# Last four tiles of a transformer and S4D layer on one core: three tiles scaled in a row, the residual sums shared out anew between VectorE and GpSimd, and the stores regrouped

## The reference

```
x = x + attention(layernorm(x))        # causal, 256 wide, with its own layernorm and residual
x = x + ffn(layernorm(x))              # first pass of the same ffn
x = x + s4d(layernorm(x))              # convolution over 512 time steps, B = 2 of them as tensor rows
x = x + ffn(layernorm(x))              # second pass

def ffn(x):                            # 256 -> 768 -> 256
    gate = silu((x @ fp8(gate_w)) * gate_scale)
    up   = (x @ fp8(up_w)) * up_scale
    return ((gate * up) @ fp8(down_w)) * down_scale
```

## Time and profile before

| | us |
|---|---|
| median of 3 runs | 124.89 (124.87 to 124.93) |
| the profiled execution | 124.83 |
| its span, first to last instruction | 123.0 |

### The profile page before, as it was taken

How to read it: one execution, slowest core, us unless ns; L and a number is a source line. 1 busy time by engine, 2 the same in 40 slices (tenths; PEclk the granted TensorE clock), 3 DMA queues, 4 the chain that set the end, 5 groups by cost and what they waited for, 6 DMA issues and landing times.

```text
span 123.0 us, 2126 instructions
## 1 busy us (share of the span) xinstructions
PE 116.2 (94%) x682; PEld 78.3 (64%) x682; DVE 96.1 (78%) x229; ACT 77.5 (63%) x147; POOL 83.7 (68%) x165
## 2 busy tenths in 40 slices
PE   5997999999999999999999999999999999999970
PEld 5885468658668758744678645667445479756650
DVE  0499999919865878768797988999899994797582
ACT  2235079695776367947966359786389666589700
POOL 2246569999999888888633388869876782037721
PEclk9999999999999999999999999999999999999997
DMA  3999930000000000000000000000000000000505
GB/s 94 302 308 365 337 101 8 0 0 0 0 0 0 3 8 0 0 0 0 0 0 0 5 0 0 0 3 5 0 0 0 3 0 5 0 0 0 171 0 171
DMA packets 5682, 5.80 MB, mean 47 GB/s; under 512 B 1140, under 2 KB 5160, under 8 KB 5672
## 3 DMA queue, kind: packets, MB, share of 16 engines
q1 hardware_dynamic: 4648, 5.52, 13.5%
q10 hardware_dynamic: 960, 0.15, 0.7%
q0 software_dynamic: 64, 0.02, 0.2%
HBM read 4.63 MB, written 1.05 MB: 46 GB/s over the span
## 4 chain that ended last, share of the span: by engine, by line
PE 60%; DVE 18%; POOL 7%; ACT 6%; issue 3%; DMA 2%; POOLq 0%; DVEq 0%; ACTq 0%
PE psum L1258 18%; PE psum L1292 10%; PE psum L1198 7%; PE psum L1173 7%; PE psum L1138 6%; DVE stats L731 5%; PE psum L1131 3%; PE psum L1272 3%; POOL rstd L301 3%; PE psum L1220 2%; DMA x_in<-in_x 2%; PE psum L1186 2%; DVE x_plus L974 2%; ACT h_rows L570 2%; DVE fused L1005 2%
## 5 line engine op out<-in xcount | busy, mean ns | idle before, releaser
L619 ACT ACTIVATE gated<-psum,scales 128x512 f32<-128x512 f32 x24 | 16.3, 681 | 12.4 <-PE psum L1258 10.2
L1292 PE MATMUL psum<-down,f_head 128*128 128x256 bf16 x96 | 22.0, 273 | 0.0
L1292 PE MATMUL psum<-down,f_tail 128*128 128x256 bf16 x96 | 22.0, 273 | 0.0
L1005 DVE SCALAR_TENSOR_TENSOR fused<-psum,up_scales_fit,gated 128x512 f32<-128x512 f32 (+1 forms) x25 | 17.8, 716 | 3.5 <-PE psum L1258 2.3
L456 POOL TENSOR_TENSOR f_tail<-fused,f_head 128x512 f16<-128x512 f32 x10 | 11.8, 1184 | 11.8 <-ACT f_head L625 10.6
L625 ACT ACTIVATE f_head<-fused 128x512 f16<-128x512 f32 (+1 forms) x25 | 15.2, 607 | 2.6 <-DVE fused L1005 2.3
L1013 DVE TENSOR_TENSOR f_tail<-fused,f_head 128x512 f16<-128x512 f32 (+1 forms) x15 | 10.2, 680 | 4.2 <-ACT f_head L625 4.2
L1258 PE MATMUL psum<-h_tail,gate 128*128 128x512 f16 x44 | 13.1, 379 | 0.0
L1258 PE MATMUL psum<-h_head,gate 128*128 128x512 f16 x44 | 13.1, 379 | 0.0
L1258 PE MATMUL psum<-h_tail,up 128*128 128x512 f16 x44 | 13.1, 379 | 0.0
L1258 PE MATMUL psum<-h_head,up 128*128 128x512 f16 x44 | 13.1, 379 | 0.0
(11 more groups left out here) (176 smaller groups left out, 265.1 us busy)
## 6 DMA issues: line engine op xcount, KB each, us to landing
x_in<-in_x SPq DMA_DIRECT2D x4, 256.0 KB, 4.4
qkv_sb<-in_qkv SPq DMA_DIRECT2D x3, 256.0 KB, 4.3
gate_raw<-in_gate_w SPq DMA_DIRECT2D x1, 768.0 KB, 6.3
up_raw<-in_up_w SPq DMA_DIRECT2D x1, 768.0 KB, 8.1
down_raw<-in_down_w SPq DMA_DIRECT2D x1, 768.0 KB, 9.7
out<-x_in SPq DMA_DIRECT2D x3, 256.0 KB, 2.1
wo_sb<-in_o_proj SPq DMA_DIRECT2D x1, 256.0 KB, 5.0
down_scale_all<-in_down_scale SPq DMA_DIRECT2D x1, 128.0 KB, 9.6
```

Source lines behind the costliest of these rows:

```text
L619: act.activation(gated[:, m % 2, :], psum[:, BANK_GATE[m % 2], :], ACT.Silu, scale=gate_scales[:, m:m + 1]).then_inc(gated_ready, 1)
L1005: dve.scalar_tensor_tensor(out=fused[:, m % FUSED, cols], in0=psum[:, BANK_UP[m % 2], cols], scalar=up_scales_fit[:, m:m + 1], in1=gated[: ...
L1292: last = pe.matmul(down_columns(n, t), part[:, m, t * P:t * P + P], down16[:, m, :], start=(m == 0 and (t % 2 == 0 or n == 2 * B - 1) and ...
```

## The change

On VectorE the third scale moves ahead of the first add, and this add is for tile 2 in place of tile 1. GpSimd adds tiles 0 and 1, each with its own wait for ScalarE's mean. On ScalarE the mean for tile 2 goes, and the mean for tile 1 is put behind `head(last, 5)`. SyncE stores tile 2 alone first, as soon as VectorE has made it, and then tiles 0 and 1 as one DMA. Tile 3 is scaled, added and stored as before. The computation is the same.

```diff
@@ SyncE
-            sp.wait_ge(x4_by_pool, T + 1)
             sp.wait_ge(x4_by_dve, 1)
+            store(slice(T + 2, T + 3))
+            sp.wait_ge(x4_by_pool, T + 2)
             store(slice(T, T + 2))
-            sp.wait_ge(x4_by_pool, T + 2)
-            store(slice(T + 2, T + 3))
             sp.wait_ge(out_stored, 16 * (K // 2 + 1))
@@ GpSimd
-            pool.wait_ge(mean_back, T + 2)
-            residual(1, x4, x3, (T, T + 2), x4_by_pool)
+            for k in (T, T + 1):
+                pool.wait_ge(mean_back, k + 1)
+                residual(1, x4, x3, (k,), x4_by_pool)
@@ ScalarE
             put_mean_back(T)
-            put_mean_back(T + 2)
             head(last, 4)
             gate(last, 5)
             head(last, 5)
+            put_mean_back(T + 1)
@@ VectorE
-            for t in (0, 1):
+            for t in (0, 1, 2):
                 ffn_scale(3 * T + t)
-            add_x3(1)
-            for t in (2, 3):
-                ffn_scale(3 * T + t)
+            add_x3(2)
+            ffn_scale(3 * T + 3)
             add_x3(3)
```

## The result

| | kernel before | changed kernel |
|---|---|---|
| runs, median us | 124.96 (12 runs of this comparison) | 125.39 (12 runs, 125.22 to 126.0) |
| changed over before | 1 | 1.0039, 95% interval 1.0023 to 1.0054 |
| profiled execution, us | 124.83 | 125.49 |
| its span, us | 123.0 | 123.7 |

On 124.89 the ratio is +0.49 us, with an interval of +0.29 to +0.67. The forecast was +0.38 us (125.27), with bounds of +0.24 to +0.45. So it is slower, and clear of no change; the size came out above the forecast and above its upper bound of 125.34.

A forecast was written before the change was run, and what follows sets the result against it. The end was taken as bounded by the last store's issue and the bytes queued before it. ScalarE 0, TensorE 0 and drain +0.38 (containing VectorE's 0.18) on 124.89 gave 125.27 us, range 124.97 to 125.42.

The forecast's parts named there:

- The stores: Final drain: tiles 0 and 1 queue behind tile 2's store, so the last byte leaves later; +0.38 us taken.
- ScalarE 0: ScalarE before head(4) and after head(5): removing one mean gains 0, and the late mean costs 0.
- VectorE by itself: VectorE's last six instructions, without neighbours: reordered, they end where they did, within 0.02 us.
- The port: VectorE's tile 2 add waits for GpSimd's second add and loses 0.39; VectorE ends 0.18 us later.
- The shared port: SBUF adds of VectorE and GpSimd: they exclude each other, and whichever starts first goes first, even 0.09 ahead.
- Rival 1: Last adds: VectorE gets the port before GpSimd's second add; +0.18 us, 125.07; chance 0.10.
- Rival 2: Final drain: bytes don't count, only the issue of the last store; +0.18 us, 125.07; chance 0.10.
- Rival 3: VectorE's last adds: 0.61 and 0.65 are their own length, no port shared; +0.18 us, 125.07; chance 0.05.
- Rival 4: Last store issued at 120.60 instead of 120.81, only its issue counting; 124.68, faster by 0.21; chance 0.05 including anything unseen below.
- The gap of two issues: SyncE's last two stores: consecutive issues start 0.49 apart at 0.47 each, so a gap of 0.04 us.

The follow-up runs named there:

- single stores: Changed kernel with tile 0 stored alone by ScalarE once made, and tile 1 alone by SyncE before tile 2; 1.0016 of the kernel before.
- the pair first: Changed kernel with SyncE's order undone, so tiles 0 and 1 are stored before tile 2; 1.0016 of the kernel before.
- 128 KB less: Changed kernel with tile 0's store left out, so SyncE's last issue carries 128 KB instead of 256; 1.0021 of the kernel before.
- VectorE first: Changed kernel with GpSimd's second sum made to wait until VectorE's first add is done; 1.0037 of the kernel before.
- split waits: Kernel before with GpSimd's last two sums each given their own wait for ScalarE's mean; 1.0007 of the kernel before.

## Where the prediction held, and which term was too small

The mechanism held: the port delays VectorE, and the stores, regrouped behind it, end later still. The step that failed is the size of the stores' term.

- **The stores: forecast +0.38 in all (bounds +0.24 to +0.45), measured +0.46, and +0.49 in the runs.** This is the term that was mis-sized. The prediction counted it in two ways and took the middle: +0.42 from the pair's issue, and +0.35 with 512 KB leaving without a gap. There is a gap: the engines' share drops to 0.47 at 121.6 to 121.7, between tile 2's data and the pair's. The pair is issued at S + 2.68 (2.72 in the sum). Its data starts about 0.96 behind its issue (120.67 to about 121.63; the sum had 0.91, from a store issued by itself), and the 384 KB took about 1.25, not 1.20. The start of 121.63 is covered in part by the end of tile 2's data; with single stores, where the second store's data begins behind a near pause, the distance is 0.95 to 0.97 as well. So the count from the pair's issue was the right one, short by 0.04, and the middle took another 0.04 off it.
- **ScalarE 0.** Held. head(4) starts at S - 3.54, as before; ScalarE sat idle for 0.42 until its input came. (The 113.33 of the prediction is the start of the two mean additions before the change, not of the activation ahead of them; with both, ScalarE was free 0.02 before head(4) began.) The late mean ended at 117.59, 1.7 before its reader.
- **VectorE by itself: no change from the order.** Held in this kernel as far as can be seen; the order alone, with the tiles as before, is worth 0.38 of VectorE's time. The prediction didn't price that case. It shows that the order by itself costs nothing here: with an add for tile 1, which needn't wait for the scale just ahead of it, VectorE starts before GpSimd's second sum.
- **The port: +0.18.** Measured +0.19. GpSimd's second sum started 0.14 ahead of VectorE's add (0.13 in the sum). With the neighbour taken away VectorE ended 0.37 earlier. That a lead this short decides is what the order of the starts suggests in every collision here; no run turned it round at the same distance.
- **The shared port.** In nine of the thirteen profiles, that of before among them, VectorE adds began inside a GpSimd sum, and each such add ended 0.27 to 0.29 behind the sum. In the three with the third scale first and the tiles as before, VectorE began first, by 0.16 to 0.17; it kept 0.47, and GpSimd took about 0.9. The rule that the prediction took from the Trainium skill (SBUF — State Buffer, section "SBUF: two separate sides"), by which the one that starts first holds the port for its whole length, agrees with all of these.
- **Rival 1** (VectorE first) didn't occur; made on purpose it gives the same time as the changed kernel. The prediction put it at +0.18, with the pair issued at S + 2.48. It went at S + 2.77: in this version GpSimd's sum ends 0.85 behind VectorE's add, while the prediction had 0.58 for a sum that waits at the port. Where a sum did wait there, with the third scale first, it ended 0.58 to 0.59 behind, so that term was right. The version tried is not quite the rival, and the rival's own price as a whole stays untested.
- **Rival 2** (bytes don't count) fell with the second sum left out, with the pair first, with 128 KB less, with VectorE first, and between the two kernels with the third scale first. The section that the prediction cites for it is on DMAs issued by GpSimd; these stores are issued by SyncE and ScalarE. **Rival 3** (the adds' own length) fell with the second sum left out. **Rival 4** needed 1 and 2 together, and neither occurred.
- **The gap of two issues.** The earlier trace rows hold two issues of 0.47 and 0.46 with their starts 0.51 apart, not 0.49; the gap of 0.04 that the sum used is right, and the two issues of the changed kernel have it.

## What to carry to other kernels

Where VectorE and GpSimd share out elementwise work on SBUF, look at which two instructions stand side by side, not only at how many each has: an add of two SBUF tensors that starts 0.14 behind GpSimd's sum cost 0.38 here, and one that started ahead of it cost nothing. At the end of a kernel count two times for the last store: its issue plus its own length (1.34 for 128 KB here), and the first byte still to go plus the time of all bytes behind it. The later of the two is the end, and a faster compute engine helps only as long as that is the first. Store each tile as soon as it is made, and never put a store that is ready behind one that isn't: this alone was 0.31 us here.

## What the runs showed of the hardware that I hadn't expected

- A GpSimd sum with a second wait ahead of it started 0.13 to 0.15 behind its releaser, and with one wait 0.08, even if the other had been met long before (split waits: 0.15, before: 0.08).
- The second of two stores that SyncE issued 0.39 to 0.41 apart took 0.43 to 0.47 to issue in place of 0.35 to 0.37, and its data began about 0.96 behind its issue in place of 0.85 to 0.91.
- A VectorE instruction at about 11 us began up to 0.9 us later from one profile to the next (10.63 before, 11.55 with split waits), and everything up to S moved with it, to 0.04. In the latest of them a weight load led the chain; that the loads are the cause is read from the chain, and no run changed them.
